# A two-layer transformer block on one core: the order of norms, statistics and inverse roots in the first layer's schedule

## The reference

```python
def _layernorm(x, axis=-1, eps=1e-05):
    m = jnp.mean(x, axis=axis, keepdims=True)
    v = jnp.var(x, axis=axis, keepdims=True)
    return (x - m) / jnp.sqrt(v + eps)
...
x = L0_attn_x
xn = _layernorm(x, axis=-1)
x = x + _L0_attn_ref(xn, ...) + _L0_ffn_ref(xn, ...)
xn = _layernorm(x, axis=-1)
x = x + _L1_attn_ref(xn, ...) + _L1_ffn_ref(xn, ...)
```

## Time and profile before

| | |
|---|---|
| Time, median of 3 runs | 1309.77 us (1308.77 to 1313.92) |
| Profiled execution | 1307.91 us, span 1306.2 us |
| Granted clock, mean | 0.946 |
| PE busy | 1104.8 us, 85% of the span |
| PE weight loads | 1004.6 us, 77% |
| DVE busy | 852.7 us, 65% |
| ScalarE busy | 688.2 us, 53% |
| GpSimd busy | 468.7 us, 36% |
| DMA moved | 166.91 MB, mean 128 GB/s |

### The profile page before, as it was taken

The page is one execution under the profiler, slowest core; times in us unless marked ns, Lnnn a source line. Parts: engine busy times, 40 slices in busy tenths (PEclk is TensorE's granted clock), DMA queues, the critical chain, the costliest instruction groups (busy, mean ns, idle before and its releaser), DMA issues.

```text
span 1306.2 us, 21769 instructions
## 1 busy us (share of the span) xinstructions
PE 1104.8 (85%) x7522; PEld 1004.6 (77%) x7522; DVE 852.7 (65%) x1642; ACT 688.2 (53%) x1918; POOL 468.7 (36%) x541
## 2 busy tenths in 40 slices
PE   0674889889879866699569999999999999999997
PEld 0463777778777754589459999999999999899996
DVE  3663568668668642498347677667776776677775
ACT  1273365456556521355136666666666666555553
POOL 6145145045235300000742343444434444488100
PEclk9996899989999977799779999999999999999999
DMA  5567476456646301756413444444444454233230
GB/s 157 103 153 160 72 201 163 96 124 195 151 91 190 101 1 56 229 161 225 159 57 113 139 128 148 152 145 124 147 127 148 127 167 125 83 113 98 65 98 17
DMA packets 150350, 166.91 MB, mean 128 GB/s; under 512 B 17921, under 2 KB 114466, under 8 KB 150178
## 3 DMA queue, kind: packets, MB, share of 16 engines
q1 hardware_dynamic: 146626, 157.12, 43.5%
q0 software_dynamic: 3616, 8.40, 2.1%
HBM read 116.70 MB, written 48.76 MB: 127 GB/s over the span
## 4 chain that ended last, share of the span: by engine, by line
PE 46%; DVE 8%; ACT 2%; another core or an unknown queue 2%; issue 1%; DMA 1%; SPq 0%; DVEq 0%
PE bank_q L1527 10%; PE ps_sa L1527 9%; PE bank_k L1527 8%; PE ps_y L1527 7%; PE ps_ta L1527 7%; PE ps_ta L1640 4%; DVE probs_a L1508 2%; ACT probs_a L1311 2%; DVE neg_max_a L1500 1%; DVE oT L1338 1%; DVE ps_sa L1506 1%; PE ps_sa L1572 1%; DMA xTa<-d_xn1T 1%; DVE h_fe L1351 0%
## 5 line engine op out<-in xcount | busy, mean ns | idle before, releaser
L1311 ACT ACTIVATE probs_a<-ps_sa,neg_max_a 128x256 f32<-128x256 f32 x256 | 117.8, 472 | 158.0 <-DVE neg_max_a L1500 154.1
L503 ACT ACTIVATE probs<-ps_s,neg_max 128x128 f32<-128x128 f32 (+1 forms) x256 | 104.7, 421 | 89.9 <-DVE neg_max L738 89.6
L1500 DVE TENSOR_REDUCE neg_max_a<-ps_sa 128x2 f32<-128x512 f32 x128 | 88.0, 691 | 71.9 <-PE ps_sa L1527 45.5
L1527 PE MATMUL bank_k<-xTa,w_qk 128*128 128x512 f32 x384 | 105.8, 410 | 14.6 <-issue 9.0
L1215 POOL CAST we_down<-raw_down_e 88x512 fp32r<-88x512 f32 x48 | 29.2, 609 | 229.1 <-DMA raw_down_e<-in_we_down 229.1
L1527 PE MATMUL bank_q<-xTa,w_qk 128*128 128x512 f32 x384 | 102.5, 400 | 9.1 <-issue 5.4
L1527 PE MATMUL ps_ta<-pTa,v 128*128 128x256 f32 x768 | 103.7, 284 | 7.3 <-issue 7.3
L511 ACT ACTIVATE pT<-ps_t 128x512 fp32r<-128x512 f32 x96 | 57.6, 600 | 92.3 <-PE ps_t L839 91.3
L1527 PE MATMUL ps_y<-w_out,oT 128*128 128x256 f32 x768 | 104.4, 286 | 1.6 <-DVE oT L1338 1.6
L1527 PE MATMUL ps_sa<-kTa,qTa 128*128 128x256 f32 x768 | 103.0, 283 | 2.4 <-DVE kTa L1338 1.6
L1527 PEld LDWEIGHTS ps_ta<-pTa,v 128*128 128x128 f32 x768 | 96.8, 190 | 7.6 <-issue 7.5
(11 more groups left out here) (250 smaller groups left out, 2852.5 us busy)
## 6 DMA issues: line engine op xcount, KB each, us to landing
w_qk<-d_w_head SPq DMA_DIRECT2D x64, 512.0 KB
raw_up<-in_we_up SPq DMA_DIRECT2D x48, 352.0 KB, 3.5
d_w_head<-parts SPq DMA_DIRECT2D x128, 128.0 KB, 2.2
raw_down_e<-in_we_down SPq DMA_DIRECT2D x48, 176.0 KB
codes<-in_w_codes SPq DMA_DIRECT2D x64, 128.0 KB, 2.5
scales<-d_scales SPq DMA_DIRECT2D x256, 32.0 KB, 2.3
q<-d_q_scr SPq DMA_DIRECT2D x24, 256.0 KB, 6.4
d_xs<-zeros SPq DMA_DIRECT2D x16, 384.0 KB, 2.8
```

The lines of the kernel that those rows point to most:

```text
L503: last = act.activation(probs[:, g % 3, a * w:(a + 1) * w], ps_s[g % 2][:, a * w:(a + 1) * w], ACT.Exp, bias=neg_max[:, g % 2, a:a + 1], s ...
L1311: last = act.activation(probs[:, s, t, :], ps_s[s][:, t * SEQ:(t + 1) * SEQ], ACT.Exp, bias=neg_max[:, s, t:t + 1], scale=1.0, accum_out=s ...
L1500: dve.tensor_reduce(neg_max[:, s, :], ps_s[s][:].rearrange("p (t k) -> p t k", t=2), AX.X, ALU.max, negate=True).then_inc(max_ok, 1)
L1527: last = pe.matmul(out, lhs[i], rhs[j], start=start and n == 0, stop=stop and n == 2, skip_group_check=True)
```

## The change

Three things are moved, and the rest follows them.

The first norm: statistics of the next turn's input from step 11 to 7, the norm from 12 to 9, and on GpSimd the root for them from behind the chunk of step 11 to ahead of the chunk of step 5 (two steps ahead of the statistics, so that GpSimd waits there). The transposes, both query projections and the first keys and values go from steps 14 to 18 to 15 to 19, and with them SP's store of the queries from 18 to 19.

The second norm: two steps behind its output product, not one (19, 21, 23); tile 3's product goes from 27 to 28 and its norm to 30. In the last turn tile 3 keeps 27 and 28.

The shared part of the next layer: it begins at step 31 instead of 29, and logit and first sum share a step, so it ends at 40 instead of 39. In the last turn it stays. `back_at` holds lists for that. SP's store of normed tiles goes from step 5 to 7.

No arithmetic is added or removed.

```diff
--- before.py
+++ after.py
@@ -303,18 +303,21 @@
             if p:
                 early[b + 4].append(("kv", p, 1))
             if p + 1 < TURNS:
-                ln_stats_at[b + 11], ln_at[b + 12] = p + 1, p + 1
+                ln_stats_at[b + 7], ln_at[b + 9] = p + 1, p + 1
                 for n, item in enumerate((("xT", p + 1, 0), ("xT", p + 1, 1), ("q", p + 1, 0), ("q", p + 1, 1), ("kv", p + 1, 0))):
-                    early[b + 14 + n].append(item)
-            for i, (n, out) in enumerate(zip(group_end, (17, 19, 21, 27))):
+                    early[b + 15 + n].append(item)
+            last = p + 1 == TURNS
+            for i, (n, out) in enumerate(zip(group_end, (17, 19, 21, 27 if last else 28))):
+                normed = out + (1 if last and i == TP - 1 else 2)
                 sums_at[b + n + 2] = (p, i)
                 late[b + n + 3].append(("ctx", p, i))
                 ctx_high_at[b + n + 4] = (p, i)
                 late[b + out].append(("out", p, i))
-                xn1_at[b + out + 1] = (p, i)
-                late[b + out + 1].append(("norm", p, i))
-            for n, item in enumerate(BACK):
-                back_at[b + 29 + n] = (p, n)
+                xn1_at[b + normed] = (p, i)
+                late[b + normed].append(("norm", p, i))
+            for n in range(len(BACK)):
+                at = b + 29 + n if last else b + 31 + n - (n > 2 * len(ST))
+                back_at.setdefault(at, []).append((p, n))
         order = front + [i for a, b in zip(early, late) for i in a + b if i[0] != "ffn" or i[2] < NF]
         NI = len(order)
         number = {item: n for n, item in enumerate(order)}
@@ -441,11 +444,11 @@
                 if n == 4 and 0 < p < TURNS - 1:
                     sp.wait_ge(x1_ok.sem, x1_ok.at(0, TP * p))
                     load_x(p + 1)
-                if n == 5 and p:
+                if n == 7 and p:
                     store_normed(p - 1)
                 if n == 17 and p:
                     store_sum(p - 1)
-                if n == 18 and p + 1 < TURNS:
+                if n == 19 and p + 1 < TURNS:
                     store_q(p + 1)
                     load_q(p + 1, 0)
             store_normed(TURNS - 1)
@@ -483,10 +486,10 @@
             inverse_root(0, TP)
             for g in range(END):
                 p, n = divmod(g, NU)
+                if g + 2 in ln_stats_at:
+                    inverse_root(0, TP)
                 if p < TURNS and n < CHUNKS:
                     split(p * CHUNKS + n)
-                if g in ln_stats_at:
-                    inverse_root(0, TP)
                 for kind, _, i in late[g]:
                     if kind == "out":
                         inverse_root(stats_of(i), 1)
@@ -570,8 +573,8 @@
                     act.activation(cT[0][:, i, :, :].rearrange("p c n -> p (c n)"), ctx_f[:], ACT.Copy).then_inc(ctx_high.sem, 1)
                 for item in early[g]:
                     early_item(item)
-                if g in back_at:
-                    shared(*back_at[g])
+                for at in back_at.get(g, ()):
+                    shared(*at)
                 if g in sums_at:
                     p, i = sums_at[g]
                     act.wait_ge(rinv_ok.sem, rinv_ok.at(0, TP * p + i + 1))
```

## The result

| | before | after |
|---|---|---|
| Time, median | 1310.73 us (1308.77 to 1313.92) | 1326.06 us (1321.08 to 1329.12) |
| Ratio | | 1.0111, 95% interval 1.007 to 1.0152 |
| Profiled execution, span | 1307.91 us, 1306.2 us | 1324.06 us, 1322.1 us |
| Granted clock, mean | 0.946 | 0.942 |
| PE busy | 1104.8 us | 1115.8 us |

What follows compares the result with a forecast made beforehand. Taken as the bound: TensorE's waits in the 460 us ahead of layer 1, whose 782 us are untouched. Gains 10 + 17 - 3 = 24 us, plus 2 for the clock: 1309.8 - 26 = 1284 us, range 1274 to 1298.

Steps and rivals of the forecast that it cites:

- Part 1: Turn 0, first norm earlier with its root ahead of chunk 5: a gain of 10 us, bounds 8 to 12.
- Check (2): Turn 0: DVE waits 4 to 7 us for tile 0's root, right behind chunk 15, and PE with it.
- the stall's 15 us: Turn 0, step 12 of before: DVE's 15.25 us wait for GpSimd's root, forecast to go, about a third returning at step 19.
- Part 2: Turns 1 and 2, the first norm's root ahead of the chunks: cost 0, with 3 us in hand.
- the chain stands 12 us: Turns 1 and 2: GpSimd holds the chunks 12 us waiting for the next input's variances; one or two come back.
- The queries' load: Behind the last chunk on SP, it lands before the next turn's scores need it: cost 0, margin 2.5 us.
- check (3): Turns 1 and 2: GpSimd idle some 12 us before chunk 21, hardly any before tile 0's root, where it had 13.9.
- Part 3: Layer 0, second norm two steps behind its product: 17 us gained from PE's waits, bounds 9 and 24.
- Part 4: Logit and first sum in one step: PE waits for DVE's logits copy, 1.0 us three times, +3 us.
- The clock: Fewer idle gaps mean less time at the lower clock level: 2 us gained, matmuls some 1.5 times as long there.
- (d): Rival: the queries' load comes late behind the last chunk on SP, next turn's scores wait; 1317 us, chance 0.05.
- (c): Rival: step 19 takes back all but 5 us of turn 0's stall, pT waits replace norm waits; 1304 us, chance 0.07.

Runs made afterwards that it cites:

- e2: After, with a buffer slot of its own for tile 0's sum in odd turns, so its residual needn't wait for the sums' store; 1315.82 us, ratio 1.0054.
- e11: e4 with the second norms of tiles 0 to 2 two steps behind their product; 1306.82 us, ratio 0.9997.
- e8: e4 with tile 0's root of turn 0 moved ahead of chunk 14 on GpSimd; ratio 0.9897 (1261.38 us, on a chip where before took 1274.97).
- e12: After, with SP issuing the store of sums and logits ahead of its work on chunk 14; 1314.43 us, ratio 1.0035.
- e1: After, with the root for the next input behind the chunk of step 7 on GpSimd in all turns; 1319.37 us, ratio 1.008.
- e4: Before, with statistics at step 7, first norm at 9, and its root ahead of the chunk of step 5 in turn 0 alone; 1304.91 us, ratio 0.9965.
- e10: e4 with logits and first sum of the shared product in one step; 1317.05 us, ratio 1.0056.
- e7: e6 with logits and first sum in one step again; ratio 1.0131 (1290.91 us, on a chip where before took 1274.97).
- e3: Before, with the first norm's part of the change alone, root ahead of the chunk in every turn; 1326.1 us, ratio 1.0115.
- e9: e3 with SP issuing the store of sums and logits ahead of its work on chunk 14; 1311.74 us, ratio 1.0016.
- e6: After, with root ahead only in turn 0, tile 3's product at 27, norm at 29, logits and first sum apart; 1273.33 us (before there 1274.97), ratio 0.9993.

## Why the prediction was wrong

**Part 1, right in its mechanism.** I had tile 0's normalisation of turn 0 at 130.1, it began at 129.95; the root of the next input stands at 87.42, where I had 88.1 to 89.1. Turn 0 gained 11.1 us for the 10 forecast. Check (2) failed in this execution: DVE shows no wait of 4 to 7 us at step 19. Part of the stall's 15 us went into steps 7, 9 and 17 (11.37 us for 7.77, at the lower clock from 111.6 on) before DVE got there. The wait is there in other executions of the same order. In e2, whose turn 0 is after's, step 17 takes 7.69 us, and DVE comes to step 19 early and waits. Timeline of e2, turn 0:

```profile
131.46 0.41 DVE L635 TENSOR_SCALAR xn_t<-x,mv,rstd 128x256 f32<-128x256 f32 x1 [4.68 <-POOL rstd L477]
```

PE's transposes behind it wait 6.95 us. In e11 DVE's wait is 4.03 us. Turn 0 has nearly the same length either way (89.1 and 88.5 us for 87.9). That fits the prediction's bound, the root behind chunk 15, and so does e8, where moving that root takes 6.1 us off the turn; the hit of 11.1 for 10 is in part luck, as the time went elsewhere than I had it.

**Part 2, the step that failed.** The hold was read rightly: "the chain stands 12 us" was 11.57 and 11.16. The queries' load makes no wait, as forecast; that its issue at 250.12, with 1.3 for it and 6.4 to landing, makes 257.8 for my 257.9 is luck. My figure is in the time of the kernel before, whose turn 1 starts 11.2 us later: counted from the turn's start I had 94.8 us and it was 106.0. The stall in step 17 held up that load and the scores that need it alike. Tile 0's root wasn't late, but check (3) held only in its first half: GpSimd stood 9.23 us before that root, because its variances waited for the store. But the sentence "Queued behind the chunks on SP are the sum's stores, stores of the new queries and their load" names three things, and only the last was worked out. The sums' store was taken at nothing, though it has a reader of its own: the residual of tile 0, in the middle of step 17, writes the buffer that it reads. In the kernel before, that store was issued 8.7 us ahead of the residual, early enough to leave no wait in the list of the earlier trace rows, so the row I looked for wasn't there. In the new order it was 7 and 6 us late; e2 and e12 show this wait alone to be the stall, and e12's turns 1 and 2, 10.2 and 6.7 us shorter than after's, put it at about 17 us; by e1 and e2 it is 10, and by the ratios of after and e12 (1.0111 and 1.0035) it is 10 too. What I had at nothing was 10 to 17.

**Part 3, the term with the wrong sign.** I counted 17 us of gain for the norm waits. They did fall, by 10.7 us over layer 0, but e11 shows the same parts in turns 1 and 2: -4.0 on the norm, +6.5 on pT. I had kept "about 0.8 of each 2.33" as the wait on pT; the rows of after show 1.55 and 1.77 with 1.14 for the norm beside them. Alone, the distance makes turns 1 and 2 4.9 and 4.3 us longer and turns 0 and 3 2.7 and 1.8 shorter (the last two are about what executions differ by); the whole is level with e4's within the intervals. The 2.76 us a turn for tile 3 weren't there either: its product in step 4 makes ScalarE's hT wait, a reader that I hadn't looked for.

**Part 4, mis-sized.** 1.0 us each; the waits were 2.71, 2.72 and 3.22, above my upper bound of 2.57, and the whole pair costs 5 to 7 us in turns 1 and 2 and 1 to 2 in turn 3 (e10, e7), because the next scores and the probabilities' transposes stand behind it on PE.

**The clock, wrong sign.** I took 2 us off for fewer gaps. After has turns 1 and 2 at 0.90 and 0.93 for 0.95 and 0.97, as the stall in each brought 13.6 us at 1.2 GHz. The factor of 1.5 was small as well: the 12 matmuls of w_down take 2.76 us there for 1.57, 1.76 times.

**The sum by what was measured** (differences of turns): turn 0 -11.1; the store's wait +16.9 (after less e12, turns 1 and 2); pair, distance and tile 3's place together +14.8 (e12 less before, turns 1 to 3: 2.7, 4.6 and 7.5), of which after has 3.1 less in turn 3. -11.1 + 16.9 + 14.8 - 3.1 = +17.5, and after's layer 0 is 17.4 longer. This is a chain of differences, so it must come out. Measured one at a time the parts don't add: the first norm with its hold in all turns +21.8 (e3 less before), the pair +15.6 (e10 less e4) and the distance +4.6 (e11 less e4) make 42. One thing that they share is seen: the residual's wait is 11.5 and 13.4 us in e3 and 6.9 and 6.05 in after, where DVE comes to it later. How much else falls together, and what tile 3's place costs, stays open.

**The rivals.** (d) had the right kind, something behind the last chunk on SP, and 1317 us, but named the queries' load and had 0.05. (c)'s second half, norm waits replaced by those on pT, is what happened, its first half isn't. The 0.88 for faster rested on one list of waits of the kernel before, and a chain that has slack isn't on such a list.

## What to carry to other kernels

Before an instruction is put ahead of others on a slow engine, follow the hold to the end of each queue behind it, and for every DMA there ask not only who reads what it brings but who may overwrite what it reads: a buffer with one copy waits for its store. Sum up the waits of a light and a heavy step together before counting one of them as gain; two pieces of work on the same PSUM bank in one step cost the wait between them and everything that PE has behind it. And give a hold only where it pays: the same root ahead of the chunk was worth a gain in turn 0 and a loss of some 14 us a turn in the others (e3 less e4).

## What the runs showed of the hardware

A stall can cost more than its length, by the clock behind it: 6.9 us of waiting PE was followed by 13.6 us at 0.50, in which the same 12 matmuls take 2.76 us for 1.57; in e9, 2.9 us of waiting went with a turn 6.6 us longer. Layer 1 took 779 to 782 us in the kernels on two chips and 746 to 748 in those on the third, and layer 0's steps agree. Most of that lies in one stretch: from 599.6 us on, 75 us of the kernel before hold 302 matmuls at a mean clock of 0.77, and the 75 us as far into layer 1 of e6, on the third chip, hold 527 at 1.00. PE stands idle there in before for some 22 us for which the profile shows no releaser; the cause is open.

The spread of the earlier trace rows goes with GpSimd's work beside it: in after the four tiles of the next input's normalisation take 2.76 us in turn 0, where GpSimd splits a chunk all the while, and 1.70 in turn 1, where GpSimd ends a chunk at 193.5 and then waits. There the first of the four takes 734 ns, the others 401 to 405:

```profile
90.58 2.76 DVE L631 TENSOR_SCALAR xn<-x_in,mv,rstd 128x256 f32<-128x256 f32 x4
90.71 0.86 POOL L480 TENSOR_TENSOR parts<-codes,scales 128x256 fp32r<-128x256 f32 x1
...
192.79 0.74 POOL L484 TENSOR_TENSOR parts<-codes,parts 128x256 fp32r<-128x256 f32 x1
192.94 1.70 DVE L631 TENSOR_SCALAR xn<-x_in,mv,rstd 128x256 f32<-128x256 f32 x4
```

The Trainium skill, GPSIMD Engine Reference, Key points, names the shared SBUF interfaces as a place where GpSimd contends with VectorE instructions that run in a 2-port mode or have two SBUF inputs. The traces agree that the two contend, with 1.1 us for four tiles of 128x256; in which mode this instruction runs they don't show.
